# A carried SSM state laid over 128 partitions: two row tiles to read it out, two column tiles to update it

## What is computed

```python
states = einsum('bclhn,bhcl,bclhp->bchpn', B, decay_states, X)   # what a chunk adds to the state
new_states = einsum('bhzc,bchpn->bzhpn', decay_chunk, states)    # carried over chunks, decayed
Y_off = einsum('bclhn,bchpn,bhcl->bclhp', C, states, state_decay_out)  # readout of the carried state
Y = Y_diag + Y_off
```

## Time and profile before

| | before |
|---|---|
| median of 3 runs | 1299.02 us (1298.74 to 1299.34) |
| the profiled execution | 1298.11 us, span of its core 1296.2 us |
| PE busy, share of the span | 1237.3 us, 95% |
| PE weight loads | 1042.1 us, 80% |
| DVE busy | 864.0 us, 67% |
| ACT busy | 618.1 us, 48% |
| POOL busy | 445.8 us, 34% |
| mean granted TensorE clock | 0.982 of full speed |
| chain that ended last | PE 86%, DVE 7%, ACT 3%, POOL 2%, issue 2% |

### The profile page before, as it was taken

One profiled execution on the slowest core, in us unless ns is written; L12 is line 12 of the kernel. 1 busy time (PEld: TensorE's weight loads), 2 busy tenths in 40 slices (PEclk: granted clock), 3 DMA queues, 4 the chain that ended last, 5 costly groups with the idle time before them and its releaser, 6 DMA issues.

```text
span 1296.2 us, 20859 instructions
## 1 busy us (share of the span) xinstructions
PE 1237.3 (95%) x7112; PEld 1042.1 (80%) x7112; DVE 864.0 (67%) x1654; ACT 618.1 (48%) x1242; POOL 445.8 (34%) x577
## 2 busy tenths in 40 slices
PE   6899999999999999999889999999999899999994
PEld 6777888888888888888757777777777688888884
DVE  4787635454443535344658888889874889999995
ACT  3443323232333323233557878787776544444441
POOL 0345100000000000000157777787775234344443
PEclk8999999999999999999979999999999899999998
DMA  4222101001010101000001001100110101111100
GB/s 179 85 78 86 33 1 33 1 1 33 1 33 1 32 0 49 0 17 1 12 17 37 26 29 38 45 27 25 36 46 17 41 2 33 32 32 32 32 17 33
DMA packets 30393, 41.29 MB, mean 32 GB/s; under 512 B 2432, under 2 KB 22912, under 8 KB 30208
## 3 DMA queue, kind: packets, MB, share of 16 engines
q1 hardware_dynamic: 30336, 40.53, 9.6%
HBM read 27.94 MB, written 12.58 MB: 31 GB/s over the span
## 4 chain that ended last, share of the span: by engine, by line
PE 86%; DVE 7%; ACT 3%; POOL 2%; issue 2%; DMA 0%; POOLq 0%; DVEq 0%; SPq 0%; ACTq 0%; PEldq 0%
PE bank L45 25%; PE bank L47 23%; PE bank L46 23%; PE bank L1825 3%; PE bank L1832 2%; PE bank L1841 2%; PE bank L1773 1%; PE bank L1807 1%; DVE mag L1083 1%; PE bank L1815 1%; PE bank L1748 1%; ACT hh L712 1%; PE bank L1725 1%; PE bank L1726 1%; DVE wf L1091 1%
## 5 line engine op out<-in xcount | busy, mean ns | idle before, releaser
L1159 DVE TENSOR_TENSOR hb<-gl,bank 128x512 f32<-128x512 f32 x128 | 87.8, 686 | 199.2 <-PE bank L47 196.6
L712 ACT ACTIVATE hh<-hb 128x512 fp32r<-128x512 f32 x128 | 80.9, 632 | 182.6 <-DVE hb L1159 182.6
L751 ACT ACTIVATE gl<-bank 128x512 f32<-128x512 f32 x128 | 76.4, 597 | 180.7 <-PE bank L47 180.6
L1122 DVE TENSOR_TENSOR hl<-hb,hh 128x512 fp32r<-128x512 f32 x128 | 95.8, 749 | 84.5 <-ACT hh L712 84.5
L695 POOL TENSOR_TENSOR dhl<-dab,dhh 128x512 fp32r<-128x512 f32 x64 | 96.5, 1529 | 141.4 <-ACT dhh L712 141.4
L540 POOL TENSOR_TENSOR veb<-mvb,eps 128x4 f32<-128x4 f32 x8 | 1.8, 228 | 377.7 <-DVE mvb L1139 377.7
L45 PE MATMUL bank<-xt_l,w_h 128*128 128x512 f32 x256 | 103.9, 406 | 7.2 <-DVE xt_l L1122 4.5
L45 PE MATMUL bank<-at_l,w_hi_a 128*128 128x512 f32 x256 | 102.5, 400 | 0.6 <-PE bank L47 0.3
L47 PE MATMUL bank<-at_h,w_hi_a 128*128 128x512 f32 x256 | 101.9, 398 | 0.0
L47 PE MATMUL bank<-xt_h,w_h 128*128 128x512 f32 x256 | 101.9, 398 | 0.0
L46 PE MATMUL bank<-xt_h,w_l 128*128 128x512 f32 x256 | 101.7, 397 | 0.0
(11 more groups left out here) (233 smaller groups left out, 3655.1 us busy)
## 6 DMA issues: line engine op xcount, KB each, us to landing
xg<-x_scratch SPq DMA_DIRECT2D x16, 512.0 KB, 4.0
xall<-in_x SPq DMA_DIRECT2D x8, 512.0 KB, 6.9
xg<-in_xt SPq DMA_DIRECT2D x8, 512.0 KB, 4.8
x_scratch<-rows_out SPq DMA_DIRECT2D x8, 512.0 KB, 3.1
x_scratch<-rows_out SPq DMA_DIRECT2D x16, 256.0 KB, 2.1
out<-rows_out SPq DMA_DIRECT2D x8, 512.0 KB, 3.2
wq<-in_codes SPq DMA_DIRECT2D x12, 256.0 KB, 2.7
sc<-in_scales SPq DMA_DIRECT2D x12, 256.0 KB, 3.0
```

The source lines that it names most:

```text
L712: return act.activation(dst, src, ACT.Copy)
L751: act.activation(gl[:, n % 2], ps_gate[n % 2][:], ACT.Gelu_apprx_tanh).then_inc(s_gelu, 1)
L1122: return dve.tensor_tensor(dst, src, hi.bitcast(F32), ALU.subtract)
L1159: dve.tensor_tensor(hb[:, n % 2], gl[:, n % 2], ps_up[n % 2][:], ALU.mult).then_inc(s_h, 1)
```

## The change

The state now lies on all 128 partitions: heads 0 and 1 on partitions 0 to 63, heads 2 and 3 on partitions 64 to 127, each half 256 columns wide.

- `y_off` becomes two matmuls with 256 columns each. The first uses array rows 0 to 63 (`ct`) and writes bank 5, columns 0 to 255; the second uses array rows 64 to 127, takes C straight from `bc` on partitions 64 to 127, and writes bank 6, columns 256 to 511.
- `state_add` keeps its 4 matmuls of 128 columns, now alternating between the two column halves of the array: head 0 to partitions 0 to 63 of bank 6, head 2 to partitions 64 to 127, then heads 1 and 3. It fills columns 0 to 255 of bank 6. Since that bank now also holds half of the readout, it gets one more wait: `c_yo`, that is, ACT has copied the readout of the same chunk.
- DVE's `new_state` is two operations of 128 partitions by 128 columns in place of four of 64 by 128.
- `et` is laid out the same way, so `decay_sums` has two matmuls of 8 columns in place of one of 16.
- ACT copies heads 2 and 3 out of bank 6. Behind the last group TensorE's wait on `c_yo` stands ahead of one MLP unit in place of behind it.

```diff
@@
+        HALF = HEADS // 2 * HEADDIM
+        yoff_of = (ps_yoff[:, 0:HALF], ps_ds[:, HALF:2 * HALF])
+
+        def rows_of(half):
+            return slice(half * D_STATE, (half + 1) * D_STATE)
@@
-        et = cs("et", [D_STATE, 2, NT, HEADS])
+        et = cs("et", [P, 2, NT, HEADS // 2])
@@
-        state = cs("state", [D_STATE, BATCH, HEADS, HEADDIM])
+        state = cs("state", [P, BATCH, HEADS // 2, HEADDIM])
@@ def decays(n, b):
-                act.activation(et[:, b].rearrange("p t h -> p (t h)"), ACS_LANE[0:D_STATE, 16:32], ACT.Exp).then_inc(c_ea, 1)
+                act.activation(et[:, b].rearrange("p t h -> p (t h)"), ACS_LANE[:, 16:24], ACT.Exp).then_inc(c_ea, 1)
@@ def y_off(s, b, k, c, u):
-                    y = act.activation(yo[:, u, h], ps_yoff[:, h * HEADDIM:(h + 1) * HEADDIM], ACT.Copy,
+                    y = act.activation(yo[:, u, h], yoff_of[h // 2][:, h % 2 * HEADDIM:(h % 2 + 1) * HEADDIM], ACT.Copy,
@@ def new_state(s, b, k, c):
-                for h in range(HEADS):
-                    st = dve.scalar_tensor_tensor(state[:, b, h], state[:, b, h], et[:, b, c, h:h + 1],
-                                                  ps_ds[0:D_STATE, h * HEADDIM:(h + 1) * HEADDIM], ALU.mult, ALU.add)
+                for j in range(HEADS // 2):
+                    st = dve.scalar_tensor_tensor(state[:, b, j], state[:, b, j], et[:, b, c, j:j + 1],
+                                                  ps_ds[:, j * HEADDIM:(j + 1) * HEADDIM], ALU.mult, ALU.add)
@@ def decay_sums(n):
-                pe.matmul(ACS_LANE[0:D_STATE, 16:32], ones[:], flat, start=True, stop=True).then_inc(c_acs, 1)
+                for half in range(2):
+                    mm = pe.matmul(ACS_LANE[rows_of(half), 16:24], ones[:], adt[:, :, 2 * half:2 * half + 2], start=True, stop=True)
+                mm.then_inc(c_acs, 1)
@@ def y_off(k, b, c):
-                pe.matmul(ps_yoff[:], ct[:, b, cols], state[:, b].rearrange("p h d -> p (h d)"),
-                          start=True, stop=True).then_inc(c_yoff, 1)
+                for half, c_rows in ((0, ct[:, b, cols]), (1, bc[rows_of(1), b, cols])):
+                    mm = pe.matmul(yoff_of[half], c_rows, state[rows_of(half), b].rearrange("p h d -> p (h d)"),
+                                   start=True, stop=True)
+                mm.then_inc(c_yoff, 1)
@@ def state_add(k, u):
+                pe.wait_ge(c_yo, k + 1 + 1)
                 pe.wait_ge(c_xsd, k + 1)
                 pe.wait_ge(c_bw, k + 1 + 1)
-                for h in range(HEADS):
-                    mm = pe.matmul(ps_ds[0:D_STATE, h * HEADDIM:(h + 1) * HEADDIM], bw[:, u, h], xsd[:, u, h],
-                                   start=True, stop=True)
+                for j in range(HEADS // 2):
+                    for half in range(2):
+                        mm = pe.matmul(ps_ds[rows_of(half), j * HEADDIM:(j + 1) * HEADDIM], bw[:, u, 2 * half + j],
+                                       xsd[:, u, 2 * half + j], start=True, stop=True)
@@
             pe.wait_ge(c_bw, NT * GROUPS + 1)
+            pe.wait_ge(c_yo, NT * GROUPS + 1)
             pe.wait_ge(c_xtk, NT * GROUPS + 1)
             unit(1, 1, 0, downs=False, front=1)
             pe.wait_ge(c_w1l, GROUPS)
-            pe.wait_ge(c_yo, NT * GROUPS + 1)
```

## The result

The changed kernel takes **1306.06 us** (median of 5 runs, 1304.68 to 1307.28) against 1299.02 us before: a ratio of 1.0054, 95% interval 1.0040 to 1.0069. It is slower by 0.54%, inside the predicted range, above its middle. The profiled execution took 1307.28 us with a span of 1305.4 us, 9.2 us longer than that of before; the mean granted clock fell from 0.982 to 0.977.

A forecast was written before the change was run, and what follows sets the result against it. TensorE was taken to bound the kernel. 1298.11 - 7.7 (readout) - 11.5 (update) + 15.5 (wait) + 1.2 (decay sums) - 0.5 (memset) + 3.4 (clock) = 1298.5, or 1299.4 us on the median's scale; range 1291 to 1317.5.

The forecast's parts named there:

- likeliest sign: Whole kernel: chance 0.57 of slower, 0.23 of faster, 0.20 of the same within about 0.2%.
- likeliest case: Whole kernel: partial overlap of array pieces, saved slots and new stall nearly cancelling, 1299.4 us (1294 to 1303), chance 0.42.
- added wait: At each step's first `state_add`, TensorE idles until ACT has copied the readout: 1.87 us in middle steps, 15.5 us in all.
- falls of the clock: Behind the stalls of TensorE: two falls of 1.7 us each, 3.4 us added, bounds 0 to 13.6.
- 3 of 4 slots for the readout: At `y_off`: one slot of 0.24 us saved in each of 32 chunks, 7.7 us, bounds 0 to 15.4.
- 5 of 8 for the update: At `state_add`: three slots of 0.12 us saved in each of 32 chunks, 11.5 us, bounds 0 to 15.4.
- rival of full overlap: Readout and update: both array pieces run side by side throughout, 30.8 us saved, 1284.4 or 1287.8 us, chance 0.10.
- None is needed sooner by TensorE: Work queued behind the stalled first update starts equally later, so the stall is not paid twice: no extra time.
- TensorE has no idle time later in the step: Rest of each step after the stall: none of the stall is given back, so no time is subtracted.
- the decay sums: At `decay_sums`: two more passes per step, 0.15 us in each of 8 steps, 1.2 us added.
- the memset: Clearing the state once, half as long per partition: half of 0.94 us, 0.5 us saved.
- relief of DVE: At `new_state`: two of four operations per chunk dropped, 21 us of DVE's time, nothing taken for it.

The follow-up runs named there:

- `g_lo` early: DVE's `g_lo` of a step's first chunk moved ahead of `dt_ratio`: 1292.92 us on the changed kernel, 1295.60 us on the kernel before.
- both moves on DVE: Changed kernel with `g_lo` ahead of `dt_ratio` and `add_out` ahead of the fourth column block's convolution: 1312.08 us; 1288.77 us with the late update.
- the best version: Changed kernel with the late update and `g_lo` early: 1271.63 us, ratio 0.9794 to the kernel before.
- the late update: Changed kernel with each step's first `state_add` moved behind other TensorE work and DVE's `new_state` moved later too: 1281.31 us, ratio 0.9868.

## Why the prediction was right and wrong

- **Range and sign** held: 1306.06 lies in 1291.0 to 1317.5, and slower was the likeliest sign. The likeliest case (no change) was wrong, and that the time comes within 6.6 us of it is luck: the array's gain was undersized by 8.0 us, and the losses (added wait, two waits on DVE, falls of the clock) by about 15.
- **The slots of the array.** Both terms failed. I took 3 of 4 slots for the readout (7.7 us) and 5 of 8 for the update (11.5 us), my estimate with passes started in written order; no run shows these slots. The traces show half in both (13.4 and 13.8): the readout's lower piece starts at 848.50, ahead of the upper one's second pass at 848.81, which is written before it, and the update written piece by piece still takes 0.59 us. The rival of full overlap had 0.10, and was held down by "It would need passes that start out of order", for which no row spoke. The loads go the same way: the eight weight loads of an update start and end within 0.42 us in place of 0.85, while its matmuls run. From 1.02 to 0.59 is four passes of 0.107 less, half of the eight, and some 0.16 us of each distance stays. That a tenth of a us is a switch between pieces was my estimate too: L1725 holds TensorE for 746.66 - 746.35 = 0.31 us ahead of L1726, on the same piece, and L1726 for 0.33 ahead of the update.
- **The added wait:** mechanism and place were right, 15.5 us predicted, 14.8 by the trace of the wait alone, one in each step and one more in the last. "A faster readout doesn't shorten this" was true and not enough: I treated the stall as fixed in length, where it is ACT's end that is fixed. With both edits it is 17.3.
- **"None is needed sooner by TensorE", "TensorE has no idle time later in the step"** held for the old array times. I read DVE's 5.8 us to spare in a step as room everywhere; at one place it had no slack against TensorE and at the other 0.34 us, where 0.85 and 0.83 are saved (0.83 and 0.74 waited). A good part of both chains is DVE waiting for POOL, which no term of the sum looked at. Missing term: 8.8 us by the trace, 10 by the runs.
- **The clock:** 3.4 us taken, bounds 0 to 13.6; some 7.7 measured. The 1.7 us a fall are half of the 3.4 us at 0.50 in the earlier trace rows, where the wait of 1.85 us has none behind it; five falls of the changed kernel cost 1.54 each. Two falls in eight stalls were an estimate. In the kernel with the wait alone a fall followed the stall of 1.80 in one of 6 steps; that of 2.2 had one in 5 of 7, in 4 of 7 with `g_lo` early and with the update written piece by piece, and in 2 of 4 with both moves on DVE. I had sized the stall at 1.87, so its growth is the likely reason of this error too; the counts are small.
- **Small edits:** the decay sums cost nothing, where 1.2 us were taken; the memset takes 0.52 us in place of 0.94, as predicted, though the wait behind it differs by more than that from kernel to kernel (3.8 us with the change, 4.8 before, 4.9 in the best version). The relief of DVE was oversized, 21 us where it is 16.2 (35.4 to 19.2 us): the operations overlap (128 of 332 ns would be 42.5 us end to end). Taking nothing for it was right for a schedule in which TensorE doesn't wait for DVE, and where it does, half of the relief is worth 1 to 2 us.

Not tried: to take away the wait by another bank for the readout's second half (as I read the kernel the other PSUM banks are in use at that time, so it would be another plan of the banks); to put ACT's copies ahead of its exponentials; to move POOL's operations out of DVE's way, which would test the reading above.

## What to carry to other kernels

Time taken off the bounding engine was kept here only where no other engine's chain had a fixed length from one of its releases to one of its waits (`g_lo` where it was cost 10 of the 24.8 us); before counting such a gain, walk through the chains that run beside the shortened stretch and write down the slack of each one. A resource shared for the sake of a faster form (here a PSUM bank) brings a wait (14.8 us by itself, 17.3 in the change); place it behind enough independent work and its whole price, clock included, goes, here 24 us for moving one call on each of two engines. And an averaged idle share of an engine says nothing of its slack at one place: DVE was idle for 5.8 us in a step, and late by 0.8 at two of its results. Part of such a chain can be a wait for a third engine that counts as busy time: look for tiny operations that take a microsecond, and at what ends just ahead of their ends.

## What the hardware showed that I had not expected

- Float32 matmuls on two row pieces (64 rows each) or two column pieces (64 columns each) run fully side by side, both passes of each: 1.05 to 0.63 us for 512 columns, 1.02 to 0.59 for four times 128.
- A matmul on a free piece starts ahead of ones written before it for the other piece: 0.59 us in either written order, with the first passes of the two pieces 0.013 us apart.
- A DVE operation of 3 or 16 columns that takes 0.15 to 0.18 us alone takes up to 1.8 us beside one of POOL (`acc` at 778.12: 1.79), and then ends 0.02 to 0.03 us after it; with the late update and `g_lo` early the same operation started 0.05 us ahead of POOL's and took 0.17.
- Four passes of 8 columns, two on each column piece, take the 0.22 us that two of 16 took.
- Stalls of 2.1 to 2.2 us had a fall to 0.50 of full speed beside their end in 15 of 26 cases over five kernels, those of 1.8 to 1.9 us in 3 of 9 over two; one such stretch was 6.8 us long, twice the usual. Waits of 1.4 to 1.9 us for `xc` have them too: the late update with both moves on DVE has three falls behind seven of them.
